# Stacks made by eight fp32 transposes, the head-norm's affine at the eviction, and a round trip through DRAM, in place of 32 fp16 transposes

## The reference, cut to what matters

```
q = _ln((x @ Wq + bq).reshape(b, s1, H, HD), qn_w, qn_b)       # norm over each head's 32 columns
k = _ln(kv[..., :HD], kn_w, kn_b)                              # 112 main keys
k_dca = _ln(kv_dca[:, :, 0], kn_dca_w, kn_dca_b)               # 16 DCA keys, their own gain and shift
ctx = _attn(q, k, v) + _attn(q, k_dca, v_dca)                  # two softmaxes
x = x + (ctx @ Wo + bo)
x = x + ffn(_layernorm(x))                                     # 8-bit fake quantisation in and out
```

## Time and profile before

| what | us |
|---|---|
| median of 3 runs (lowest, highest) | 451.85 (449.41, 453.16) |
| the profiled execution | 451.91 |
| its span | 450.0 |
| PE busy | 355.6 (79%) |
| DVE busy | 353.0 (78%) |
| ACT busy | 220.3 (49%) |
| POOL busy | 229.8 (51%) |
| mean granted TensorE clock | 0.947 |
| bytes moved by DMA | 23.46 MB |

### The profile page before, as it was taken

The page is one execution under the profiler, slowest core; times in us unless marked ns, Lnnn a source line. Parts: engine busy times, 40 slices in busy tenths (PEclk is TensorE's granted clock), DMA queues, the critical chain, the costliest instruction groups (busy, mean ns, idle before and its releaser), DMA issues. The chain is left out here.

```text
span 450.0 us, 8358 instructions
## 1 busy us (share of the span) xinstructions
PE 355.6 (79%) x2759; PEld 279.8 (62%) x2759; DVE 353.0 (78%) x904; ACT 220.3 (49%) x381; POOL 229.8 (51%) x273
## 2 busy tenths in 40 slices
PE   0065776869999999999999999999898989767842
PEld 0023644567777676777777777777777768656620
DVE  0395376667898989898989898989999997987642
ACT  0123434263747473838383738383838383634402
POOL 8231041351738383929292929383838474554411
PEclk9997876898999999999999999999999999998975
DMA  7904110010010202030202030201020110100001
GB/s 264 334 18 148 39 40 0 1 42 25 16 50 1 90 1 89 1 88 2 89 1 89 1 90 13 76 27 62 28 63 27 63 47 9 50 1 23 3 23 47
DMA packets 18534, 23.46 MB, mean 52 GB/s; under 512 B 6968, under 2 KB 9276, under 8 KB 18492
## 3 DMA queue, kind: packets, MB, share of 16 engines
q1 hardware_dynamic: 16960, 21.51, 14.7%
q10 hardware_dynamic: 1532, 1.42, 1.0%
...
## 5 line engine op out<-in xcount | busy, mean ns | idle before, releaser
L408 POOL TENSOR_TENSOR wkv_raw<-wq_raw,k_gain 128x512 f32<-128x512 f32 x16 | 21.3, 1332 | 131.4 <-DVE wq_raw L895 131.4
L1096 PE MATMUL bank<-v_aug,prob_store 128*128 128x66 f32 x512 | 68.1, 276 | 7.8 <-DVE seg_out L809 7.1
L1096 PEld LDWEIGHTS bank<-v_aug,prob_store 128*128 128x128 f32 x512 | 63.8, 193 | 12.0 <-ACT prob_store L553 6.7
L553 ACT ACTIVATE prob_store<-bank,exp_scale 128x512 f32<-128x512 f32 x64 | 42.1, 683 | 27.8 <-PE bank L1079 27.7
L796 DVE TENSOR_REDUCE neg_max<-bank 128x4 f32<-128x448 f32 (+1 forms) x128 | 45.1, 414 | 8.1 <-PE bank L1067 7.7
L424 POOL TENSOR_TENSOR kv_dca<-seg_out 128x128 f32<-128x128 f32 x64 | 39.0, 618 | 12.0 <-DVE seg_out L809 10.2
L484 ACT ACTIVATE k_stack<-bank 128x1024 f16<-128x1024 f16 x32 | 31.0, 1021 | 7.8 <-PE bank L1103 7.7
L1078 PE MATMUL bank<-q_stack,k_stack 128*128 128x128 f16 x256 | 33.9, 220 | 0.7 <-ACT maxT L484 0.7
L1079 PE MATMUL bank<-maxT,sel 128*128 128x128 bf16 x256 | 33.7, 219 | 0.0
L484 ACT ACTIVATE maxT<-bank 128x128 bf16<-128x128 bf16 x16 | 4.4, 277 | 58.3 <-PE bank L1147 58.3
L1007 PE MATMUL bank<-wo_hi,cT_hi 128*128 128x512 f32 x64 | 27.2, 424 | 6.2 <-DVE cT_lo L828 6.2
...
## 6 DMA issues: line engine op xcount, KB each, us to landing
x_in<-in_x SPq DMA_DIRECT2D x16, 256.0 KB, 2.8
out<-kv_dca SPq DMA_DIRECT2D x16, 256.0 KB, 2.0
...
y_dcaT<-in_x SPq DMA_DIRECT2D x8, 256.0 KB, 3.1
x_res<-in_x SPq DMA_DIRECT2D x8, 256.0 KB, 3.0
...
```

The lines of the kernel that those rows point to most:

```text
L553: s.activation(flat(probs[:, gr % 2]), bank[4 + gr % 2][:, :], ACT.Exp, scale=exp_scale[:, 0:1]).then_inc(probs_ready.sem, 1)
L1096: last = mm(bank[6 + gr % 2][:, VW * h:VW * (h + 1)], probs[:, gr % 2, h], v_aug[:, Bt.parity, HG * gr + h], start=True, stop=True)
```

## The change

What it does:

- The Newton steps, k_t and q_t move on VectorE to a place between `maxima(0)` and `maxima(1)`.
- TensorE transposes k_t (112 rows) and q_t in fp32, four [128, 128] blocks each, behind scores 3. In that layout a column of gain or shift lies along partitions, so ScalarE applies both as scale and bias when it evicts the bank, twice for each of k and q: once to fp32, once to fp16 (`normed`).
- POOL subtracts the fp16 part from the fp32 value (`low`). `affine` on POOL, `low` and `double` on VectorE, the 32 fp16 transposes and the four stack evictions go.
- SyncE stores the four parts to DRAM (128 KB each) and loads them back in eight DMAs of 128 KB, each into the 32 partitions of one slot (`spread`). Bt's first scores wait for these loads. The layout of a stack becomes [128, 4, 4, 128].
- The DCA keys are normalised once in setup, and POOL copies 16 columns of them a batch; their load into k_raw goes, as does their half of the DRAM scratch.
- In setup, the FFN kernel's column maxima are taken with one reduction and four transposes instead of 16 transposes and four reductions, ahead of t = 0 instead of t = −1; its quantisation moves from the step of t = −1 into that of t = 0.
- POOL's rounding for D stands ahead of that for C; small FFN steps on VectorE change places.

```diff
-        q_stack = sb("q_stack", [P, 2, H, P], FP16)
-        k_stack = sb("k_stack", [P, 2, H, P], FP16)
+        q_hi, q_lo = sb("q_hi", [P, XC, P], FP16), sb("q_lo", [P, XC, P], FP16)
+        k_hi, k_lo = sb("k_hi", [P, XC, P], FP16), sb("k_lo", [P, XC, P], FP16)
+        q_stack = sb("q_stack", [P, 2, HG, XC, P], FP16)
+        k_stack = sb("k_stack", [P, 2, HG, XC, P], FP16)
...
+            def spread(N, stack, which, parts, landed):
+                for slot, part in enumerate(parts):
+                    sp.dma_start(stack[HD * slot:HD * (slot + 1), N.parity].rearrange("p g c n -> p g (c n)"),
+                                 stack_scratch[N.parity, which, part].rearrange("(g d) n -> d g n", d=HD)
+                                 ).then_inc(landed.sem(N), 16)
+            def flat(t):
+                return t.rearrange("p c n -> p (c n)")
...
+                    sp.wait_ge(*khi_ready.of(N))
+                    sp.wait_ge(*dcacols_ready.of(N))
+                    sp.dma_start(put[0, 0], flat(k_hi[:])).then_inc(k_put.sem, 16)
+                    sp.wait_ge(*klo_ready.of(N))
+                    sp.dma_start(put[0, 1], flat(k_lo[:])).then_inc(k_put.sem, 16)
+                    sp.wait_ge(*qhi_ready.of(N))
+                    sp.dma_start(put[1, 0], flat(q_hi[:])).then_inc(q_put.sem, 16)
+                    sp.wait_ge(*qlo_ready.of(N))
+                    sp.dma_start(put[1, 1], flat(q_lo[:])).then_inc(q_put.sem, 16)
+                    if N.has(2):
+                        sp.wait_ge(*shifted_ready.of(N.back(2)))
+                    sp.wait_ge(*k_put.of(N))
+                    spread(N, k_stack, 0, (0, 1, 0, 1), kstack_in)
+                    sp.wait_ge(*q_put.of(N))
+                    spread(N, q_stack, 1, (0, 0, 1, 1), qstack_in)
...
-                def affine(between, tile_t, tile_w, tile_n, gain, shift, t_ready, w_ready, hi_used, lo_used, n_ready):
-                    pool.wait_ge(*t_ready.of(N))
-                    g.tensor_tensor(tile_w, tile_t, gain[:], ALU.mult).then_inc(w_ready.sem, 1)
-                    if between is not None:
-                        between()
-                    pool.wait_ge(*w_ready.of(N))
+                def low(lo, n, hi, n_ready, hi_ready, put, done, keys):
+                    pool.wait_ge(*n_ready.of(N))
+                    pool.wait_ge(*hi_ready.of(N))
                     if N.has(1):
-                        pool.wait_ge(*hi_used.of(N.back(1)))
-                        pool.wait_ge(*lo_used.of(N.back(1)))
-                    g.tensor_tensor(tile_n, tile_w, shift[:], ALU.add).then_inc(n_ready.sem, 1)
+                        pool.wait_ge(*put.of(N.back(1)))
+                    g.tensor_tensor(lo[:, :, 0:keys], blocks(n)[:, :, 0:keys], hi[:, :, 0:keys], ALU.subtract
+                                    ).then_inc(done.sem, 1)
+                def dca_columns():
+                    if N.has(1):
+                        pool.wait_ge(*k_put.of(N.back(1)))
+                    cols = slice(DCA * N.index(), DCA * (N.index() + 1))
+                    g.tensor_copy(k_hi[:, :, MAIN:P], kdca_hi[:, :, cols]).then_inc(dcacols_ready.sem, 1)
...
+                    if N.has(1):
+                        dca_columns()
+                    low(k_lo, k_n, k_hi, kn_ready, khi_ready, k_put, klo_ready, MAIN)
+                    low(q_lo, q_n, q_hi, qn_ready, qhi_ready, q_put, qlo_ready, P)
                     if N.first():
-                        pool.wait_ge(gains_ready.sem, 4)
-                        pool.wait_ge(wlo_ready.sem, 5)
...
-                    affine(centred, k_t, k_w, k_n, k_gain, k_shift, kt_ready, kw_ready, khi_ready, klo_ready, kn_ready)
+                        for j in range(2):
...
+                centred()
+                if D is not None:
...
                 act.wait_ge(wq_centred.sem, 1)
                 copy(wq_hi[:], wq_raw[:]).then_inc(whi_ready.sem, 1)
...
                 copy(wo_hi[:], wo_raw[:]).then_inc(whi_ready.sem, 1)
+                act.wait_ge(dcass_ready.sem, 1)
+                s.activation(dca_small[:, 1], dca_small[:, 0], ACT.Ln).then_inc(dcaln_ready.sem, 1)
+                act.wait_ge(dcaln_ready.sem, 1)
...
-                def high_part(n_ready, used, parts, src, done):
-                    act.wait_ge(*n_ready.of(N))
+                def normed(T_ready, bk, keys, first_col, n, n_ready, lo_done, hi, hi_ready, put):
+                    if N.first():
+                        act.wait_ge(affine_ready.sem, 2)
+                    act.wait_ge(*T_ready.of(N))
                     if N.has(1):
-                        act.wait_ge(*used.of(N.back(1)))
-                    copy(parts[:, :, 0], src.rearrange("p (h d) -> p h d", d=HD)).then_inc(done.sem, 1)
-                def stacked(T_ready, stack, half, bk, done):
-                    act.wait_ge(*T_ready.of(N, half + 1))
-                    if N.has(2):
-                        act.wait_ge(*shifted_ready.of(N.back(2)))
-                    copy(flat(stack[:, N.parity, 8 * half:8 * half + 8]), bank[bk][:, :].bitcast(FP16)
-                         ).then_inc(done.sem, 1)
+                        act.wait_ge(*lo_done.of(N.back(1)))
+                        act.wait_ge(*put.of(N.back(1)))
+                    src = bank[bk][:, :].rearrange("p (c n) -> p c n", n=P)[:, :, 0:keys]
+                    gain, shift = affine[:, first_col:first_col + 1], affine[:, first_col + 1:first_col + 2]
+                    s.activation(n.rearrange("p (c n) -> p c n", n=P)[:, :, 0:keys], src, ACT.Identity, bias=shift,
+                                 scale=gain).then_inc(n_ready.sem, 1)
+                    s.activation(hi[:, :, 0:keys], src, ACT.Identity, bias=shift, scale=gain).then_inc(hi_ready.sem, 1)
                 if N is not None:
                     rsqrt(qk_small[:, 1], qk_small[:, 2], qk_small[:, 0], head_steps, head_ln, head_exp, N, 1)
...
+                if N is not None:
+                    normed(kT_ready, 2, MAIN, 2, k_n, kn_ready, klo_ready, k_hi, khi_ready, k_put)
+                    normed(qT_ready, 3, P, 0, q_n, qn_ready, qlo_ready, q_hi, qhi_ready, q_put)
+                    if N.first():
+                        setup_dca()
...
+            def setup_squares():
...
+                dve.wait_ge(dcasq_ready.sem, 1)
+                link(v.tensor_reduce(dca_ss[:], dca_sq.rearrange("p j (h d) -> p j h d", d=HD), AX.X, ALU.add))
+                v.tensor_scalar(dca_small[:, 0], dca_ss[:], 1.0 / HD, HEAD_EPS, ALU.mult, ALU.add
+                                ).then_inc(dcass_ready.sem, 1)
+            def setup_dca():
+                dve.wait_ge(dcaexp_ready.sem, 1)
+                link(newton(1, dca_small[:, 0], dca_small[:, 2], dca_small[:, 3]))
+                link(newton(2, dca_small[:, 3], dca_small[:, 2], dca_small[:, 4]))
+                link(newton(3, dca_small[:, 4], dca_small[:, 2], dca_small[:, 5]))
+                for j in range(2):
+                    v.tensor_tensor(grouped(dca_t[:, j]), grouped(kv_dca[:, j, 0]), wide(dca_small[:, 5, j]), ALU.mult
+                                    ).then_inc(dcat_ready.sem, 1)
+            def setup_columns():
+                dve.wait_ge(fk_in.sem, 16)
+                v.tensor_reduce(fk_abs, fk_raw[:].rearrange("p c n -> p n c"), AX.X, ALU.max, apply_absolute_value=True
+                                ).then_inc(fkabs_ready.sem, 1)
             def setup_maxima():
                 dve.wait_ge(fkT_ready.sem, 1)
-                for c in range(XC):
-                    v.tensor_reduce(fk_cols[:, 0, c:c + 1], bank[4 + c][:, :], AX.X, ALU.max,
-                                    apply_absolute_value=True).then_inc(fkmax_ready.sem, 1)
-                dve.wait_ge(fkmax_ready.sem, XC)
+                link(v.tensor_reduce(fk_cols[:, 0], bank[7][:, :].rearrange("p (c n) -> p c n", n=P), AX.X, ALU.max))
...
                 if Bt is not None:
                     maxima(0)
+                if N is not None:
+                    dve.wait_ge(*head_exp.of(N))
+                    newton(1, qk_small[:, 0], qk_small[:, 2], qk_small[:, 3]).then_inc(head_steps.sem, 1)
+                    dve.wait_ge(*head_steps.of(N, 2))
+                    newton(2, qk_small[:, 3], qk_small[:, 2], qk_small[:, 4]).then_inc(head_steps.sem, 1)
+                    dve.wait_ge(*head_steps.of(N, 3))
+                    newton(3, qk_small[:, 4], qk_small[:, 2], qk_small[:, 5]).then_inc(head_steps.sem, 1)
+                    dve.wait_ge(*head_steps.of(N, 4))
+                    if N.has(1):
+                        dve.wait_ge(*kT_ready.of(N.back(1)))
+                    v.tensor_tensor(grouped(k_t[0:MAIN]), grouped(k_raw[0:MAIN, N.parity]),
+                                    wide(qk_small[0:MAIN, 5, 1]), ALU.mult).then_inc(kt_ready.sem, 1)
+                    if N.has(1):
+                        dve.wait_ge(*qT_ready.of(N.back(1)))
```

(74 more changed lines are left out.)

305 lines of the change are left out of this document (129 added, 176 removed).

## The result

The changed kernel takes 468.64 us (median of 4 runs, 467.66 to 469.32); the ratio to the kernel before is 1.038, with a 95% interval of 1.032 to 1.044. The direction and the mechanism of the steady steps held; the time lies 0.6 us above its range of 454 to 468 (0.2 above the 468.4 from which its top is rounded). The profiled execution has a span of 466.5 us against 450.0, and a mean granted clock of 0.901 against 0.947.

The account below looks back on a forecast made before the run. VectorE was taken to pace the step by a little, TensorE following closely. From 451.9 us, 13 steps at −0.1 + 1.04 gave +12.2 and the ends −4.3: 460 us, range 454 to 468, whole range 438 to 468.

Parts of the forecast that it names:

- the step t = 0: First full step: the FFN quantisation delays xT_lo by some 6 us, but old waits go; net 0.
- the falling clock: Half clock behind TensorE's new stall: 1.3 us in four steps of five, 1.04 a step; bounds nothing and 1.7.
- What bounds it, and the moved steps: VectorE's chain to the second maxima holds TensorE: waits 0.8 and 2.1 us, fourth scores at 4.6, projection at 5.68.
- A step without a fall: Full step with the clock kept: 21.99 + 2.82 − 2.93 = 21.9 us, −0.1 a step.
- VectorE's relief: VectorE's busy share should drop by about 3 us a step, with a wait ahead of f_z.
- Ends: Outside the 13 full steps: setup −1.8, between −5 and +3, step at 390.43 −2.5; sum −4.3 us.
- The range: Forecast's own range 454 to 468 us, its top from 1.6 us more in each of 13 steps; whole range 438 to 468.
- DMA: Round trip through DRAM: last q load lands at 18.7 of 21.9 us, costing nothing, with 3.2 us of cover.
- The clock stays: Rival: the stall comes but TensorE's clock stays up, giving 444.8 us; chance 0.20.
- The chain is shorter: Rival: head scalar and result run uncontended on VectorE, the stall loses 0.6 us, giving 437 us; chance 0.13.

Follow-up runs that it names:

- (3): Changed kernel with one more VectorE pass of 512 elements, result unused, between q_t and the second maxima: 482.93 us, ratio 1.066 to the kernel before.
- (2): Changed kernel with x_plus computed ahead of the first combine on POOL instead of behind x_norm: 455.51 us, ratio 1.006 to the kernel before.
- (7): Changed kernel with VectorE's second maxima and low parts ahead of the Newton steps, and TensorE's k and q transposes behind the output projection: 424.72 us, ratio 0.945.
- 11: Changed kernel with TensorE's k and q transposes behind the output projection and xT_lo right behind yT_lo; second maxima not moved: 475.50 us, ratio 1.055.
- 12: Kernel before the change with x_plus computed ahead of the first combine on POOL: 473.03 us, ratio 1.049 to the kernel before.
- Kernel 4: Changed kernel without the DRAM round trip of later batches, which reuse the first two batches' stacks: 469.72 us, ratio 1.037 to the kernel before.
- 9: Changed kernel with four extra bf16 matmuls on TensorE in the wait ahead of the fourth scores: 461.17 us, ratio 1.021 to the kernel before.
- Kernel 5: Changed kernel with the FFN kernel's quantisation moved to just ahead of the first normalise of the same step: 465.93 us, ratio 1.033 to the kernel before.
- kernel 1: Changed kernel with eight extra bf16 matmuls on TensorE in the wait ahead of the fourth scores: 451.09 us, ratio 0.996 to the kernel before.
- kernel 10: Changed kernel with eight extra matmuls ahead of the fourth scores and x_plus ahead of the first combine: 443.56 us, ratio 0.983 to the kernel before.

## Why the prediction failed by its size, point by point

Two terms of the sum failed by their size: the step t = 0, put at 0, is +3.3 us, and the falling clock, put at 1.04 us a step, cost 11 × 1.57 / 13 = 1.33, so that the 13 steps grow by 16.2 for 12.2. The range's upper end covered the second and not the first: with +3.3 in it, its top would have been 471.7.

**What bounds it, and the moved steps: right.** TensorE waits ahead of the third and the fourth scores, and everything is behind them. Predicted: fourth scores at 4.6, projection at 5.68. Measured: 5.08, and 6.07 without a fall. The difference is the head scalar, 1.29 for 0.54, less 0.26 at its start (246.21 − 245.82 = 0.39 for 0.65). The prediction's own figures held a sign of it: x_plus from 0.1 for 1.7 us covers the head scalar's start at 0.65, and before the change the head scalar ended (258.58 + 0.54 = 259.12) as x_plus did (257.37 + 1.71 = 259.08); its 0.54 was the rest of that pass. k_t and q_t took 0.69 each, uncontended, as taken. Lengthening (3), shortening (2) and taking away the gate (7) moved the step as this reading says.

**A step without a fall: right.** Predicted 21.9, measured 21.97. Two small errors nearly cancel, which is luck: the projection starts 0.4 later, and the rest of the step is 15.90 instead of 16.20. Two slips of the working (1.46 for 6 × 0.24 = 1.44, and 1.22 for −1.75 + 0.80 + 0.91 + 0.71 + 0.57 = 1.24) change it by 0.06 at most.

**VectorE's relief: a sign that failed.** The busy time was to drop by about 3 us a step; it drops from 20.03 to 19.09. Passes that now run beside POOL are longer: besides the head scalar, the maxima's second part (L937) takes 1.03 us under POOL's first subtraction (253.28 to 254.32) and 0.19 in kernels 7 and 11, where it does not meet one. TensorE doesn't wait for that pass in the steps shown, so it costs the step nothing.

**The price of a fall, mis-sized.** I took 1.3, for a part of the slow stretch hidden in the stall, in four of five steps: 1.04 a step. It is 1.57 in the changed kernel, in 11 steps of 13, as in 12 and in four steps of 2. Some falls cost more: steps of 24.00, 24.39 and 24.79 in kernels 2, 4 and 9, with a mean clock of 0.86, are 2.4 to 2.8 above those without. Nearly none of the slow stretch lies in the stall. The 13 steps cost 16.2 us, not 12.2. My upper end of 1.6 in each step covered that.

**The first full step (t = 0): put at nothing, the step that failed.** "0", for the quantisation that moves into it, against old waits that go. It is +3.3. I had noted that xT_lo comes some 6 us later and followed it no further: to the q product that waits 2.91 us for it, to the half clock that goes on until 97.5, to the first weighting. Kernel 5 takes 4.7 us off this step by moving that block alone, and is then 1.4 below the step of before: so the old waits that go are worth 1.4, and the block costs 4.7.

**Ends.** Setup −0.9 (predicted −1.8), the step at t = 14 −1.2 (−2.5), the rest behind it −0.9 (0). The step at t = 14 takes 20.43 with a mean clock of 0.83, and 18.12 at 1.00 in kernel 1: it has a fall of its own, which I had not counted. In all 16.2 + 3.3 − 0.9 − 1.2 − 0.9 = 16.5, the difference of the spans; predicted 7.9. Of the 8.6 between, 4.0 is in the 13 steps, nearly all of it the clock's price, 3.3 the step t = 0, and 1.3 the other ends.

**The range.** Its top, 468.4, was the clock's worst case on top of ends of −4.3, held fixed. I had written bounds of −5 to +3 for the setup alone and used none of them. With them the top would have been above 470.

**DMA: right.** SyncE's queue issues the q stack's four loads of the same step as here:

```profile
259.63 1.73 SPq L311 DMA_DIRECT2D q_stack<-stack_scratch  x4
```

The last goes out at 261.4, a load lands in 3.1 us (median of the 64 q loads), and the next first scores are at 269.4: 5 us of cover against 3.2 predicted. Kernel 4 shows that without the transfers nothing changes.

**The rivals.** "The clock stays" needed 444.8: kernel 1 makes it stay and is at 0.996, 450, as the ends are not −5.8 (of which −1.5 had no source). The prediction leaned on the place at 402.95, where the clock stayed up for 2.4 us behind a wait of 2.10. TensorE's timeline of the kernel before has the next wait there:

```profile
405.39 1.75 PE L1096 MATMUL bank<-v_aug,prob_store 128*128 128x66 f32 x8 [1.14 <-DVE seg_out L809]
```

Behind it the granted clock is 0.56 from 405.30 to 408.00. So that place is one where two waits, 2.10 and 1.14 us, ended in a fall, and spoke against this rival.

"The chain is shorter" would have needed the head scalar uncontended; kernel 10, with both, is at 443.6. No kernel here was at 437.
